# Gathering each stretch of 16 edge chunks once, in one stage with keys, values, counts and node updates

## What is computed

```python
edge_index = jnp.stack([src, dst])
xn = _layernorm(x, axis=-1)
...
# graph convolution on xn
summed = jax.ops.segment_sum(x[src], dst, num_segments=n)
deg = jax.ops.segment_sum(jnp.ones_like(src, dtype=x.dtype), dst, num_segments=n)
agg = summed / jnp.maximum(deg, 1.0)[:, None]
out = jnp.concatenate([x, agg], axis=-1) @ weight
out = out / jnp.linalg.norm(out, axis=-1, keepdims=True)
return out + bias
...
# linear attention on xn: 8 heads of 64; k and v normalized in each head
dots = jnp.einsum('bhnd,bhne->bhde', k, v)
out = jnp.einsum('bhnd,bhde->bhne', q, dots) / n
...
x = x + _L0_gnn_ref(xn, edge_index, ...) + _L0_mix_ref(xn[None], ...)[0]
x = x + _L0_ffn_ref(_layernorm(x, axis=-1)[None], ..., L0_ffn_edge_index)[0]
```

## Time and profile before

| | us |
|---|---|
| time before, median of 3 runs | 5516.6 (5515.82 to 5516.77) |
| the profiled execution, its own time | 5518.46 |
| its span in the trace | 5516.7 |
| block plan | 0 to 55.8 |
| block sort | 55.8 to 323.2 |
| block keys and values | 323.2 to 978 |
| block mixing and places | 978 to 996 |
| block gather | 996 to 3432.8 |
| block experts | 3432.8 to 5516.7 |

### The profile page before, as it was taken

One profiled execution on the slowest core, in us unless ns is written; L12 is line 12 of the kernel. 1 busy time (PEld: TensorE's weight loads), 2 busy tenths in 40 slices (PEclk: granted clock), 3 DMA queues, 4 the chain that ended last, 5 costly groups with the idle time before them and its releaser, 6 DMA issues. The chain is left out here.

```text
span 5516.7 us, 54436 instructions
## 1 busy us (share of the span) xinstructions
PE 3910.3 (71%) x13646; PEld 2436.2 (44%) x13647; DVE 2157.5 (39%) x5008; ACT 752.0 (14%) x1704; POOL 3185.4 (58%) x3234
## 2 busy tenths in 40 slices
PE   0169998677778877788777776999699798876000
PEld 0135554344444544455444444666465455544000
DVE  8789999222222222222222222021212121213566
ACT  0024442000000000000000000211112122211000
POOL 0012221577777777777777775666666666665510
PEclk9999998677777787777778777999899899988555
DMA  2012221344444444444444444122222222222566
GB/s 69 0 43 67 67 66 36 92 122 125 121 121 120 125 124 122 122 120 123 123 122 121 119 123 116 42 80 54 56 62 63 54 60 54 60 54 67 153 202 215
DMA packets 375205, 521.99 MB, mean 95 GB/s; under 512 B 147535, under 2 KB 286727, under 8 KB 374980
## 3 DMA queue, kind: packets, MB, share of 16 engines
q0 software_dynamic: 126528, 254.64, 18.5%
q1 hardware_dynamic: 248579, 266.19, 15.3%
HBM read 386.56 MB, written 133.06 MB: 94 GB/s over the span
## 5 line engine op out<-in xcount | busy, mean ns | idle before, releaser
L889 POOL DMA_INDIRECT rows<-xn_rows,gix x1818 | 1835.4, 1010 | 582.1 <-issue 545.2
L1012 PE MATMUL PS<-rows,oh 128*125 128x257 f32 x3636 | 1438.8, 521 | 543.5 <-DMA rows<-xn_rows,gix 534.5
L1012 PEld LDWEIGHTS PS<-rows,oh 128*125 128x125 f32 x3636 | 742.0, 237 | 1204.2 <-DMA rows<-xn_rows,gix 1057.7
L1208 POOL DMA_INDIRECT nb<-route_rows,idx x1024 | 1000.9, 977 | 464.9 <-issue 464.9
L1510 PE MATMUL PS<-x2g,arena 128*128 128x500 f32 x1600 | 699.8, 598 | 193.0 <-ACT hid L1481 175.4
L1520 PE MATMUL PS<-arena,hid 128*125 128x256 f32 x3200 | 703.1, 382 | 26.4 <-ACT hid L1481 19.2
L922 DVE TENSOR_TENSOR oh<-iota_j,rel 128x1125 f32<-128x1125 f32 x202 | 269.4, 1334 | 1116.8 <-PE PS L1012 1107.9
L1520 PEld LDWEIGHTS PS<-arena,hid 128*125 128x125 f32 x3200 | 601.9, 189 | 137.7 <-ACT hid L1481 39.4
L1510 PEld LDWEIGHTS PS<-x2g,arena 128*128 128x128 f32 x1600 | 312.1, 196 | 566.5 <-issue 382.6
L577 POOL TENSOR_TENSOR fold<-sq 125x512 f32<-125x512 f32 x100 | 133.4, 1334 | 724.0 <-ACT sq L649 724.0
L1459 DVE TENSOR_TENSOR y_sb<-PS,b_b 125x512 f32<-125x512 f32 x200 | 127.9, 685 | 1067.4 <-PE PS L1520 1067.4
(11 more groups left out here) (311 smaller groups left out, 3429.0 us busy)
## 6 DMA issues: line engine op xcount, KB each, us to landing
y_rows<-y_sb SPq DMA_DIRECT2D x100, 512.0 KB, 2.9
y_in<-y_rows SPq DMA_DIRECT2D x100, 512.0 KB, 3.5
rows<-xn_rows,gix POOLq DMA_INDIRECT x1818, 2.8
nb<-route_rows,idx POOLq DMA_INDIRECT x1024
x_rows<-x SPq DMA_DIRECT2D x100, 128.0 KB, 3.7
x_in<-x_rows SPq DMA_DIRECT2D x100, 128.0 KB, 4.7
x_in<-in_x SPq DMA_DIRECT2D x100, 125.0 KB
xn_rows<-x_n SPq DMA_DIRECT2D x100, 125.0 KB
```

The costliest lines, as they stand in the source:

```text
L889: pool.indirect_dma_start(out=rows[h][:, q, 0:D], out_offset=None, in_=xn_rows, in_offset=bass.IndirectOffsetOnAxis(ap=gix[h][:, q:q + 1], ...
L1012: last = mm(SUM[u][0:NP, 0:D + 1], oh[h][:, q, :], rows[h][:, q, :], start=False, stop=False)
L1208: pool.indirect_dma_start(out=nb[b % NBUF][:, c, :], out_offset=None, in_=route_rows, in_offset=bass.IndirectOffsetOnAxis(ap=idx[:, b * W ...
```

## The change

- **Plan.** The chunks are cut into 104 spans of `GU` = 16, whatever tile they belong to. Per span the smallest node (`neg_node`) and the step from the span before (`step`) are kept. The per-tile plan is gone, and with it ScalarE's part. A guard is added: where a span reaches over more than 128 nodes, or the order of the spans doesn't fit, a slow loop over chunks and tiles (`add_again`) runs behind the sort and its sums are taken. In these inputs no span reaches over more than 126 nodes.
- **Sort.** The first normalization of all rows now runs beside the sort, in 7 batches of 14 x 128 rows: ScalarE sums and squares (98 times each), VectorE takes a reciprocal (`first_norm`), GpSimd scales 98 tiles of 128 x 256, and SyncE writes `xn_rows`. Both copies behind a turn are VectorE's.
- **One block** takes the place of keys and values, mixing and places, and gather. `walk` lays all of it out over half spans s (8 chunks): the products of half span s, keys and values of tile s - 2, counting step s, and from half span 112 on the node updates of tile s - 112 to s - 118. Four halves are in flight instead of two. A span's sums go from `SUM` to `kept` (ScalarE) and from there to `sum_rows` in memory; the next span adds the row of the node on the border (`at_first`). `mean` reads a tile's sums back from `sum_rows`.
- The pairwise addition on GpSimd is gone; `spread` sums 125 x 1024 squares.
- `w1` is loaded in this block and no longer in the experts' block.

```diff
-GU = 18
+GU = 16
+HU = GU // 2
+SPANS = GC // GU
+QUAD = 4
...
+NS = 2 * SPANS
+MIX_AT = NT + 3
+HISTS = FC // 8
+POST_AT = 2 * SPANS + 4 - NT
...
+def walk(eng, last, stages):
+
+    on = lambda s: tuple(begin <= s - lag < end for lag, begin, end, _ in stages)
+
+    def half(s, i):
+        for works, (lag, _, _, emit) in zip(on(s), stages):
+            if works:
+                k = s - lag
+                emit(k + i * 4, k // 2 + i * 2, k % 2, k // 2 % 2)
...
+                for b in range(LN_BATCHES):
+                    pool.wait_ge(s_rs, b + 1)
+                    for j in range(b * LB, (b + 1) * LB):
+                        nc.gpsimd.tensor_scalar(x_all[:, j, :], x_all[:, j, :], nm[:, j:j + 1], rs[:, j:j + 1],
+                                                ALU.add, ALU.mult).then_inc(s_xo, 1)
...
                     v.tensor_copy(keys[(k + 1) % 2][:, 0:512], TR[0][:, :])
-                    dve.wait_ge(s_cp, trip + 1)
+                    dve.wait_ge(s_ps, 2 * trip + 2)
+                    v.tensor_copy(keys[(k + 1) % 2][:, 512:1024], TR[1][:, :])
...
+                for s in range(NS):
+                    g, h, w = s // 2, s % 2, s // 2 % 2
+                    pool.wait_ge(s_used[h], g + 1)
+                    for q in range(HU):
+                        pool.indirect_dma_start(out=rows[w][h][:, q, 0:D], out_offset=None, in_=xn_rows,
+                                                in_offset=bass.IndirectOffsetOnAxis(ap=gsrc[:, s * HU + q:s * HU + q + 1], axis=0)
+                                                ).then_inc(s_rows[w][(h * HU + q) // QUAD], 16)
...
+                def one_hot(s, g, h, w):
+                    v.drain()
+                    v.tensor_scalar(rel[h][:], gdst[:, bass.ds(s * HU, HU)], neg_node[:, bass.ds(g, 1)], None, ALU.add)
+                    v.drain()
+                    dve.wait_ge(s_used[h], g + 1)
+                    if h == 0:
+                        v.tensor_tensor(at_first[w][:], step[:, bass.ds(g, 1)], iota_p[:], ALU.is_equal)
+                    v.tensor_tensor(oh[w][h][:], iota_j[:].rearrange("p (o n) -> p o n", o=1).broadcast_to([P, HU, P]),
+                                    along(rel[h][:], P), ALU.is_equal).then_inc(s_ohr[h], 1)
...
+                def spread(j, _, u, w):
+                    dve.wait_ge(s_sq, j + 1)
+                    v.tensor_reduce(ss[u][:], sq[:].rearrange("p s (h e) -> p (s h) e", e=DH), AX.X, ALU.add).then_inc(s_ss, 1)
...
+                walk(dve, POST_AT + NT + 7, [
+                    (3, 0, NT, values), (POST_AT + 6, 0, NT, router_row), (POST_AT + 3, 0, NT, residual), (0, 0, HISTS, hist),
+                    (POST_AT + 3, 0, NT, second_norm), (2, 0, NT, spread), (MIX_AT, 0, 1, mixed), (PLACES_AT, 0, 1, places),
+                    (-1, 1, NS, one_hot), (POST_AT, 0, NT, mean)])
...
+                walk(act, POST_AT + NT + 7, [
+                    (0, 0, NS, keep_sums), (3, 0, NT, roots), (2, 0, NT, squares), (1, 0, NT, turn_copy),
+                    (POST_AT + 2, 0, NT, norms), (POST_AT + 3, 0, NT, std), (POST_AT + 1, 0, NT, turn_mean), (POST_AT + 4, 0, NT, turn_x2)])
...
+                def sums(s, g, h, w):
+                    if h == 0:
+                        pe.wait_ge(s_kept, g + 1)
+                    pe.wait_ge(s_ohr[h], g + 1)
+                    for q in range(HU):
+                        if q % QUAD == 0:
+                            pe.wait_ge(s_rows[w][(h * HU + q) // QUAD], (g - w) * 8 * QUAD + 16 * QUAD)
+                        last = mm(SUM[:, 0:D + 1], oh[w][h][:, q, :], rows[w][h][:, q, :], start=h == 0 and q == 0, stop=h == 1 and q == HU - 1)
+                    if h == 0:
+                        last = mm(SUM[0:1, 0:D + 1], at_first[w][:], kept[1 - w][:], start=False, stop=False)
+                    last.then_inc(s_used[h], 1)
...
+                walk(pe, POST_AT + NT + 7, [
+                    (0, 0, NS, sums), (2, 0, NT, keys_values), (1, 0, NT, turn), (3, 0, NT, outer), (POST_AT + 2, 0, NT, linear),
+                    (POST_AT + 1, 0, NT, turn_mean), (POST_AT + 4, 0, NT, turn_x2), (POST_AT + 5, 0, NT, router), (0, 0, HISTS, count_nodes),
+                    (MIX_AT, 0, 1, mixed), (PLACES_AT, 0, 1, places)])
```

More of the change, by code:

```diff
@@ L50 @@
 FG = NT // FT
-def steps(eng, n, unroll, stages):
-    depth = max(lag for lag, _ in stages)
-    head = -(-depth // unroll) * unroll
-    body = (n - head) // unroll
-    def step(s, slot, static):
-        for lag, emit in stages:
-            if static is None or 0 <= static - lag < n:
-                emit(s - lag, (slot - lag) % unroll)
-    for s in range(head):
-        step(s, s % unroll, s)
-    with eng.Fori(0, body) as i:
-        for u in range(unroll):
-            step(i * unroll + (head + u), u, None)
-    for s in range(head + body * unroll, n + depth):
-        step(s, s % unroll, s)
+NS = 2 * SPANS
+MIX_AT = NT + 3
+HISTS = FC // 8
+POST_AT = 2 * SPANS + 4 - NT
+SPANS_AT = SPANS - NT // 2
+PLACES_AT = HISTS + 4
+LN_TILES = -(-N // P)
+LB = 14
+LN_FIRST, LN_STEP = 28, 12
+LN_BATCHES = LN_TILES // LB
+LN_LEFT = N - (LN_TILES - 1) * P
+def walk(eng, last, stages):
[5 more added lines that the diff above has]
+                emit(k + i * 4, k // 2 + i * 2, k % 2, k // 2 % 2)
+    s = 0
+    while s < last:
+        n = s
+        while n + 4 <= last and all(on(n + u) == on(s) for u in range(4)):
+            n += 4
+        if n - s >= 8:
+            with eng.Fori(0, (n - s) // 4) as i:
+                for u in range(4):
+                    half(s + u, i)
+            s = n
+        else:
+            for u in range(4):
+                half(s + u, 0)
+            s += 4
 def wait_after(eng, sem, value):
@@ new lines, in _ @@
+                no_less(SPANS - 1, lambda to: v.tensor_scalar(to, step[:, 1:SPANS], -1.0, float(P), ALU.mult, ALU.add))
+                no_less(SPANS, lambda to: v.scalar_tensor_tensor(out=to, in0=node_lo, scalar=float(P - 1), in1=node_hi,
+                                                                 op0=ALU.add, op1=ALU.subtract))
+                for u in range(2):
+                    n = min(NT // 2, SPANS - SPANS_AT - u)
+                    no_less(n, lambda to: v.tensor_tensor(to, node_lo[:, SPANS_AT + u:SPANS_AT + u + n],
+                                                          neg_first[:, u + 1:u + 2 * n:2], ALU.add))
@@ L534, in build @@
-            s_xs = [ev(f"s_xs{u}") for u in range(2)]
-            s_ts = [ev(f"s_ts{u}") for u in range(2)]
-            s_var = ev("s_var")
-            s_std = ev("s_std")
-            s_xn = ev("s_xn")
+            ring = lambda name, shape, dt=f32: [[one(f"{name}{w}{h}", shape, dt) for h in range(2)] for w in range(2)]
+            rows, oh = ring("rows", [P, HU, D + 1]), ring("oh", [P, HU, P])
+            rel = [one(f"rel{h}", [P, HU]) for h in range(2)]
+            at_first, kept = two("at_first", [P, 1]), two("kept", [P, D + 1])
@@ new lines, in build @@
+            from_s, last_s, some, spare = (one(n, [NT, NP]) for n in ("from_s", "last_s", "some", "spare"))
+            s_t, p_t, x_in = two("s_t", [P, 2 * NP]), two("p_t", [P, 2 * NP]), two("x_in", [NP, D])
+            ssq, rstd = two("ssq", [NP, 1]), two("rstd", [NP, 1])
+            gsq = one("gsq", [NP, D])
+            x1, x2, x2_t = two("x1", [P, D]), two("x2", [NP, D]), two("x2_t", [P, 2 * NP])
+            st6, mv, rt = two("st6", [NP, 6]), two("mv", [NP, 2]), two("rt", [NP, ROW])
+            nothing = one("nothing", [P, REC])
@@ L813, in build @@
+            s_w2 = ev("s_w2")
+            s_pl = [ev(f"s_plx{u}") for u in range(2)]
             s_st = ev("s_st")
             s_stc = ev("s_stc")
[L815 removed]
             s_lin = ev("s_lin")
@@ new lines, in mixed @@
+                def mixed(_, t, u, w):
+                    zero(DT[:, :], P, 512, start=False, stop=True).then_inc(s_mixp, 1)
+                    pe.wait_ge(s_mixd, 1)
+                    for q in range(4):
+                        last = mm(UP[q // 2][:, (q % 2) * D:(q % 2 + 1) * D], dt_sb[:, q, :], wo[:, q, :], start=True, stop=True)
+                        if q % 2:
+                            last.then_inc(s_mixp, 1)
+                    pe.wait_ge(s_mixd, 3)
+                    for k in range(2):
+                        for q in range(4):
+                            last = mm(MP[:, k * D:(k + 1) * D], wq[:, q, k * P:(k + 1) * P], u_sb[:, q, :], start=q == 0, stop=q == 3)
+                    last.then_inc(s_mixp, 1)
+                    pe.wait_ge(s_mixd, 4)
```

822 lines of the change are left out of this document (388 added, 434 removed).

## The result

The changed kernel takes 5141.6 us (median of 4 runs, 5135.2 to 5148.0) against 5516.2 before: ratio 0.9321, interval 0.9305 to 0.9337. The forecast was 5100, with a range of 4740 to 5310.

The account below looks back on a forecast made before the run. Stages had different limits: TensorE in keys and values, GpSimd in the gather block. 2445 us outside the new block plus 2656 in it, including 200 for TensorE's clock, gave 5101 us; range 4740 to 5310.

Parts of the forecast that it names:

- The chain: New block: dependent work through TensorE, ScalarE and VectorE sets the pace, 12.1 us per half span with keys, 11.0 with node updates.
- Rival 2: New block: GpSimd sets the pace, 11.0 and 10.5 us per half span; 4751 us, or 4583 without holds; chance 0.08.
- The clock's term: New block: TensorE's pauses lower its clock, 1.7 us lost in each of 196 cycles, weighted 0.6: +200 us.
- rival 3: New block: every TensorE pause costs its clock loss in full, +333 us, 5234 in all; chance 0.17.
- Rival 1: New block: TensorE's clock stays up and pauses cost nothing, 4901 us in all; chance 0.20.
- The sort's term: Sort: 98 scalings on GpSimd, 0.46 us each, all exclusive with VectorE: +45 us, bounds +20 to +75.
- rows 8: Profile rows before the change: a counting one-hot beside GpSimd's addition took 1.76 instead of 0.67 us, read as GpSimd holding VectorE.
- The middle and the ends: New block: 12 half spans without keys at GpSimd's 11.0 us, 132 us; a start of 3 us and a tail of 55.
- The holds of gathers: New block: VectorE's one-hots delay GpSimd's gathers, raising a half span from 10.0 to 11.0 us with keys, 10.5 with node updates.
- rows 4: Timeline before the change: a gather begun at 1517.96 inside VectorE's one-hot takes 2.00 us, read as lasting until that one-hot ends.

Follow-up runs that it names:

- the first two experiments: The changed kernel with VectorE's one-hot moved first in each step, 4796.3 us; and with it moved just ahead of `spread`, 4858.1 us.
- the filler: The changed kernel with nine products of zeros on TensorE behind each half span's counting while keys run: 4985.9 us, ratio 0.9048.
- the first four experiments: On the changed kernel: one-hot first, 4796.3 us; one-hot ahead of `spread`, 4858.1; products of zeros behind counting, 4985.9; half span's products last on TensorE, 4786.9.
- the last one: The changed kernel with one-hot behind `hist` while keys run, first on VectorE from half span 112, `x_in` and `p_t` loaded behind the residual: 5512.1 us, ratio 0.8377.
- the short scaling: The changed kernel with GpSimd scaling 128 x 1 in place of 128 x 256 elements, 98 times beside the sort: 5750.5 us.

## Why the prediction held, and where it was off

| | forecast | measured |
|---|---|---|
| plan | 46.8 | 48.8 |
| sort | 312.4 and 2 | 276.6 |
| start and half spans with keys, to the 102nd one-hot | 1327 | 1384.7 |
| the next 12 | 132 | 95.3 |
| the next 94, with node updates | 1130 | 1155.9 |
| from the 208th one-hot to the end of the block | 67 | 88.1 |
| experts | 2083.9 | 2083.9 |
| sum | 5101 | 5133.4 |

**The chain was right, in its members and its size.** At full clock, with the pause filled, a half span with keys takes 12.02 us, forecast 12.1. One with node updates, with the 1.7 us of lost clock taken off, is 12.30 - 1.7 = 10.6, forecast 11.0; that all of this loss lies on its chain is not shown. That the one-hot closes both chains the first two experiments show, and that TensorE would not wait for rows the changed kernel's own waits. Rival 2 (GpSimd's pace) is what the kernel with the one-hot first reaches while keys run, at the price forecast for it, 11.0 us; with node updates it stays above GpSimd's 10.4 because of the load of `p_t`.

**The clock's term was undersized.** I took 0.6 of 1.7 us for each cycle because the shorter pauses might cost nothing. The pauses were longer than worked out (2.6 to 3.2 us in place of 2.2 with keys: TensorE's `turn`, `outer` and counting take 1.7 us together, not 2.1, and the chain's links some tenths more), and nearly every one cost: 1.62 us by the filler with keys, 1.7 by the window with node updates. For 196 half spans that is an estimate of 100 x 1.62 + 96 x 1.7 = 325 us in place of 200. That is rival 3 (every pause in full), in its mechanism and at about its price, 333. The total came out below rival 3's 5234 because the sort, the middle and the chain with node updates were shorter than forecast. The filler shows that it is the pause. Rival 1 (the clock stays up) falls by the windows: 0.86 over the block, where the forecast said 0.75 to 0.9. The page of the Trainium skill named with it ("TensorE: Matmul & The Clock Gate", section "HAM oscillation — how this bites in real kernels") has the case of short groups with a wait behind each, longer than the group. The windows here agree in the outcome, a next group that runs at the lower level, though some 11 us of work stand ahead of each pause of 2.6 to 3.2 us. Its advice to group the products did not keep the clock up here, since one pause for each group was left.

**The sort's term was wrong in its mechanism.** 45 us were forecast, the whole scaling as time that VectorE loses, with 0.46 us for each operation. An operation takes 1.08 us, more than twice that, and costs the sort 0.06. The sort grew by 9.2 us in all; the other 3.5 were not separated. The step that failed is the one from rows 8: one counting one-hot that was held by GpSimd's addition of two tensors was taken for a rule of all operations on both engines. Had the exclusion held, the true length would have cost 104.6 us: the two errors worked against each other.

**The middle and the ends.** After the last half span with keys GpSimd's four full halves are there already, and twelve half spans take 7.94 us each, not GpSimd's 11.0: 37 us too much. The start is slower, 62.0 us for the first four, where rows are waited for, and the tail, eleven steps without gathers where the prediction counted seven, takes 88 in place of 67. The deviations of the sort and the middle (-73) and those of the half spans and the ends (+105) left +32 of 5133: part of the closeness is luck.

**The holds of gathers** stood in the forecast at 1.0 us for a half span with keys, in bounds that the chain covered. In the changed kernel they are off the path. Where GpSimd sets the pace they show: 1.08 or 0.61 by the order of VectorE's work, 0.07 where no operation has two tensors. The prediction's reading of rows 4 was inexact: the gather of 1517.96 ends at 1519.96, 0.82 us behind the one-hot's end at 1519.14, and not with it. All 188 gathers of the kernel before that begin inside a two-input one-hot of VectorE, and not at its edges, end 0.81 to 0.82 us behind its end, whatever was left of it: the gather stands until the operation is over and then does nearly all of its own 0.95 us. The Trainium skill ("SBUF — State Buffer", section "Who interferes with whom") has a two-input operation of VectorE contend with a GpSimd instruction that reads SBUF, and not with one that only writes it. The prediction's rival 2 took a gather for one that only writes descriptors, and the measured holds (1022 against 955 ns in the mean) speak against that case. But a gather also reads its indices from `gsrc`, in SBUF, and by that the page's rule would agree with the holds; no run separates the two.

## What to carry over

When stages of several engines are laid into one loop, follow one turn of it through all engines: an operation that the next turn needs first, such as the one-hot here, must not stand behind one that waits for this turn's last result; moving it cost nothing and was worth 345 us. A short pause of TensorE in every turn can cost more than the time in which it stands, since the slow clock falls on the work right behind it (here 1.6 us behind each pause of 2.9); fill it or remove it, and read the granted clock in windows of one us. When an operation leaves the chain, look at once for the next circle, here loads and stores queued on SyncE behind a wait; and read in each stretch anew who waits for whom, since one pace near GpSimd's was GpSimd's own (11.04) and the other was not (11.18).

## What was not expected of the hardware

- GpSimd's scaling by two scalars for each partition takes 854 ns for 128 x 1 and 1082 ns for 128 x 256 elements: nearly all of it is not in the elements.
- Useless products made the kernel faster: 1.9 us of products of zeros on TensorE for each half span, 156 us less in all.
- A gather of GpSimd that begins inside a two-input operation of VectorE ends 0.82 us behind that operation's end, so it loses what was left of the operation, up to some 1.05 us.
- Some groups of runs were slower as a whole, with instructions at their usual durations: the kernel before takes 6590.7 and 6641.6 us there, and 5510 to 5516 in the others. It isn't shown to be the chip: the first four experiments (5515.8) and the last one (6641.6) ran on a chip of the same number, 11. Nor does it cost the same everywhere. The changed kernel with the short scaling takes 13.66 us for a half span with keys, as the changed kernel elsewhere (13.64), but 12.91 in place of 12.30 with node updates; the kernel with the one-hot behind `hist` takes 11.96 in place of 10.58 and 12.88 in place of 12.02. In its experts' block TensorE stands 143 times for 0.5 to 1.2 us (0.84 in the middle) before a product, with no releaser, and the same kernel elsewhere never does:

```profile
4043.25 0.58 PE L1571 MATMUL PS<-arena,hid 128*125 128x256 f32 x1 [0.86 <-issue]
```

Why isn't known.
